# A top-64 attention kernel: exponentials behind the counts, the guess and the moments earlier, a third head copied later

## The reference

```
Q = (layernorm(x) @ Wq.T + bq) by head;  K, V = (ctx @ W.T + b) by head
scores = Q K^T / sqrt(16)
topk_scores, topk_idx = top_k(scores, 64)
attn = softmax(topk_scores) @ V[topk_idx]
x = x + tanh(g_xattn) * (attn @ Wo.T + bo)
x = x + tanh(g_ffn) * (fp8_gemm(layernorm(x)) + bias)
```

## Time and profile before

| | us |
|---|---|
| median of 3 runs | 3224.66 (3223.86 to 3225.97) |
| the profiled execution | 3223.62 |
| its span | 3221.7 |
| VectorE busy | 2552.6 |
| ScalarE busy | 2501.8 |
| TensorE matmul busy | 1510.1 |
| GpSimd busy | 979.2 |

### The profile page before, as it was taken

The page is one execution under the profiler, slowest core; times in us unless marked ns, Lnnn a source line. Parts: engine busy times, 40 slices in busy tenths (PEclk is TensorE's granted clock), DMA queues, the critical chain, the costliest instruction groups (busy, mean ns, idle before and its releaser), DMA issues. The chain is left out here.

```text
span 3221.7 us, 56352 instructions
## 1 busy us (share of the span) xinstructions
PE 1510.1 (47%) x9104; PEld 971.1 (30%) x9104; DVE 2552.6 (79%) x10774; ACT 2501.8 (78%) x8774; POOL 979.2 (30%) x1204
## 2 busy tenths in 40 slices
PE   3244545455444545533545445544454355444442
PEld 2132333233233333322323233323233233232221
DVE  2688788788888788788878888887878887888884
ACT  1777888788888888866888788888788688687892
POOL 6223233223323233322233233223333223232112
PEclk8565666666666666665666666666566666566666
DMA  3223332223333223332223333232333123322211
GB/s 71 47 36 54 57 59 51 49 49 59 64 54 48 55 52 59 55 53 41 49 51 64 54 54 55 53 56 51 63 54 60 34 52 57 53 48 41 41 35 36
DMA packets 451929, 166.76 MB, mean 52 GB/s; under 512 B 245616, under 2 KB 451440, under 8 KB 451520
## 3 DMA queue, kind: packets, MB, share of 16 engines
q1 hardware_dynamic: 451136, 162.38, 28.5%
q0 software_dynamic: 384, 0.33, 0.1%
HBM read 102.57 MB, written 59.24 MB: 50 GB/s over the span
## 5 line engine op out<-in xcount | busy, mean ns | idle before, releaser
L970 ACT ACTIVATE act_junk<-score_sb,X 128x256 int8<-128x256 f32 x3072 | 1521.6, 511 | 52.6 <-DVE X L1272 49.0
L970 ACT ACTIVATION_READ_ACCUMULATOR act_junk<-score_sb,X 128x1 f32 x3072 | 627.7, 204 | 0.0
L1014 ACT ACTIVATE pT_sb<-ps_e 128x512 f32<-128x512 f32 x512 | 304.6, 596 | 400.0 <-PE ps_e L775 400.0
L757 PE MATMUL ps_s<-ks,qs 96*128 96x256 bf16 x1024 | 244.4, 365 | 729.4 <-DVE score_sb L1178 716.8
L1005 ACT ACTIVATE unfit<-score_sb,thr 128x256 bf16<-128x256 f32 x1024 | 430.4, 507 | 149.2 <-DVEq L1443 149.2
L771 PE MATMUL ps_e<-qs,ks 99*128 99x256 bf16 x1024 | 365.4, 365 | 311.2 <-ACT unfit L1005 217.4
L1178 DVE TENSOR_SCALAR_CACHE_REDUCE score_sb<-ps_s 128x256 f32<-128x256 f32 x1024 | 398.1, 411 | 13.4 <-PE ps_s L757 7.8
L775 PE MATMUL ps_e<-dropb,unfit 128*128 128x128 bf16 x2048 | 367.6, 279 | 0.0
L792 PE MATMUL ps_o<-pT_sb,v_aug 128*32 128x256 f32 x2048 | 293.3, 503 | 157.6 <-ACT o_sb L1021 153.2
L567 POOL CAST split<-proj 128x512 bf16<-128x512 f32 x64 | 39.8, 622 | 1000.4 <-ACT proj L954 999.8
L757 PEld LDWEIGHTS ps_s<-ks,qs 96*128 96x128 bf16 x1024 | 100.6, 121 | 782.6 <-DVE score_sb L1178 757.9
(11 more groups left out here) (181 smaller groups left out, 3902.4 us busy)
## 6 DMA issues: line engine op xcount, KB each, us to landing
rows<-q_scr SPq DMA_DIRECT2D x192, 128.0 KB, 5.0
rows<-k_scr SPq DMA_DIRECT2D x192, 128.0 KB, 4.9
o_scr<-o_sb SPq DMA_DIRECT2D x128, 128.0 KB, 2.8
q_scr<-split SPq DMA_DIRECT2D x32, 384.0 KB, 2.7
k_scr<-split SPq DMA_DIRECT2D x32, 384.0 KB, 2.7
x_in<-in_x SPq DMA_DIRECT2D x32, 256.0 KB, 2.8
ctx_sb<-in_ctx SPq DMA_DIRECT2D x32, 256.0 KB, 3.0
v_scr<-proj SPq DMA_DIRECT2D x32, 256.0 KB, 5.9
```

The costliest lines, as they stand in the source:

```text
L757: ins = nc.tensor.matmul(ps_s[:, n % 2, jh * TOK:(jh + 1) * TOK], qs[u][0:SPLITS, h, 8 * jh:8 * jh + 8, :].rearrange("d j t -> d (j t)"), ...
L970: ins = nc.scalar.activation(act_junk[:, t % JUNK, :], score_sb[:, slot, t, :], ACT.Sign, scale=-1.0, bias=X[slot % 2][:, 0, t:t + 1], acc ...
L1014: nc.scalar.activation(pT_sb[:, n % QUAD, :], ps_e[:, n % 2, :], ACT.Exp).then_inc(s_PT, 1)
```

## The change

Four pieces of work move; none is added or removed.

- ScalarE: each third of the counts stands ahead of the round's exponential instead of behind it. The moments are evacuated behind the first third (and its exponential) of round (0,0) instead of behind all three; the guess behind the second third of round 1 instead of ahead of the last third of round 2.
- TensorE: the products of the guess are issued in round 1 instead of round 2, and wait for the moments' evacuation, since both use ps_b. `front_transposes`, which also writes ps_b, waits for the guess's evacuation.
- VectorE: in rounds 0 and 1 the third head's scores are copied behind the update of the thresholds.

```
             def front_transposes(b, taken, estimated):
                 pe.wait_ge(s_xn[0], b + 1)
                 pe.wait_ge(s_mo, taken)
+                pe.wait_ge(s_ge, estimated)
...
                 pe.wait_ge(s_ge, 2 * b + g)
+                pe.wait_ge(s_mo, b + 1)
...
-                        if has(1) and r == 2:
-                            gauss(b + 1, (u + 1) % OPS, g, 2 * b + 6 if has(2) else 2 * NB,
-                                  2 * b + 4 + 2 * g if has(2) else 2 * NB)
+                        if has(1) and r == 1:
+                            gauss(b + 1, (u + 1) % OPS, g, 2 * b + 4, 2 * b + 4 + 2 * g if has(2) else 2 * NB)
...
-                            front_transposes(b + 2, b + 2)
+                            front_transposes(b + 2, b + 2, 2 * b + 3)
...
                     for r in range(GUIDES):
                         for k in range(3):
+                            if guided:
+                                guide_counts(2 * b + g + 1, (2 * p + g + 1) % RING, r, THIRDS[k])
                             if k < len(HEADS[r]):
                                 taken(HEADS[r][k])
-                            elif has(1):
+                            if has(1) and (g, r, k) == (0, 0, 0):
+                                evacuate_moments(b + 1)
+                            if has(1) and (r, k) == (1, 1):
                                 evacuate_gauss(2 * (b + 1) + g)
-                            if guided:
-                                guide_counts(2 * b + g + 1, (2 * p + g + 1) % RING, r, THIRDS[k])
-                        if has(1) and (g, r) == (0, 0):
-                            evacuate_moments(b + 1)
...
                         next(finals)
-                        if not last:
-                            copy(HEADS[r][2], 0)
-                            copy(HEADS[r][2], 1)
                         next(finals, None)
...
                         for _ in steps:
                             pass
+                        if not last:
+                            copy(HEADS[r][2], 0)
+                            copy(HEADS[r][2], 1)
```

More of the change, by code:

```diff
@@ L685, in _, with front_transposes @@
             pe.wait_ge(s_wev, 4)
-            def front_transposes(b, taken):
+            def front_transposes(b, taken, estimated):
                 pe.wait_ge(s_xn[0], b + 1)
                 pe.wait_ge(s_mo, taken)
+                pe.wait_ge(s_ge, estimated)
                 pe.wait_ge(s_ctx, 16 * b + 16)
@@ L835, in _ @@
             for b in range(2):
-                front_transposes(b, 0)
+                front_transposes(b, 0, 0)
                 project(b, 0, 0)
```

## The result

| | before | after |
|---|---|---|
| median, us | 3224.26 (3223.49 to 3225.97, 4 runs) | 3030.81 (3025.43 to 3034.51, 4 runs) |
| ratio | | 0.9398 (0.9382 to 0.9414) |
| span of the profiled execution | 3221.7 | 3032.6 |
| VectorE busy | 2552.6 | 2576.4 |
| VectorE idle (span less busy) | 669.1 | 456.2 |

The change makes the kernel 6.0% faster, 194 us. The prediction's sum was 242 us, to 2983 us, in a range of 2945 to 3090 that holds the measured time. In the two profiled executions VectorE's idle time is 213 us less and its busy time 24 us more.

A forecast was written before the change was run, and what follows sets the result against it. VectorE (79% busy) and ScalarE (78%) were taken to be bound by how they hand work to one another. 99.5 + 81 + 82 - 20 = 242 us saved gives 2983 us; 8 in 10 range 2945 to 3090.

The forecast's parts named there:

- (a): Moments evacuated behind the first third of round (0,0): VectorE's wait for them goes, 99.5 us gained.
- (b): Guess made in the second round instead of the third: VectorE's wait for it goes, less its own handover, 81 us.
- (c): ScalarE's exponentials behind each third of the counts: the last count comes 3.69 + 0.5 us earlier in (0,0).
- The waits for counts: VectorE's waits for ScalarE's counts: 2.7 us a batch go, in 30 batches 82 us.
- my table: One batch followed stretch by stretch in the new order: period 82 us, some 0.9 us of count wait left in (0,2).
- (d): Third head's copy behind the update: new X 0.7 us sooner in four of six rounds, VectorE's own work unchanged.
- Contention: VectorE slowed by GpSimd working beside it: costs 20 us, with bounds of nothing and 60 us.
- the main case: 74% for 2983 us, from 2945 (no contention and no wait left) to 3030 (contention 60).
- Slower: Rival, 5%: later exponentials delay TensorE's first scores of a round, 2 us in each of six rounds, giving 3299 us.
- another ring: Rival, 3%: the keys' projection through ScalarE, GpSimd and DRAM holds the period at 91.6 us; nothing changes, 3224 us.
- Most holes only move: Rival, 18%: waits for ps_e stay on ScalarE behind the counts, so ScalarE sets the period, 86 us a batch; 3073 us.
- the sign against the forecast: ScalarE without a hole in (1,0) and (1,1) while VectorE waits for counts there would show the forecast wrong.

The follow-up runs named there:

- the load on ScalarE: The changed kernel with three of eight exponentials of a half made twice on ScalarE: 3084.97 us, 0.9559 of the kernel before.
- the run with the moves exchanged: The changed kernel with GpSimd's spreading copy in four and, on SyncE, the output's moves ahead of the value rows' moves: 3014.16 us, 0.9334.
- the split kernel: The changed kernel with GpSimd's spreading of an operand by head made as four copies of a quarter: 3013.67 us, 0.9338 of the kernel before.

## Why the prediction was right, and where its sizes were off

- **What bounds the kernel.** Right: the two engines held each other up over ps_e and the moments. The single largest part, by itself 161 us, is the order of counts and exponentials.
- **(a) The moments.** Right: 99.5 us forecast, 98.9 us gone from the wait, 92 us alone.
- **(b) The guess.** The wait went by 81.3 us (idle before `variance`, all causes, 125.2 to 43.9), as forecast. That it is a gain of its own was wrong: alone it gave 8 us, and 55 of the 81 go with (c) alone (125.2 to 70.0). Behind (c), moments and guess together took another 51 us of idle time away (`key_var` 46.0 to 21.2, `variance` 70.0 to 43.9) and gave 19 us back before `X`; in time they are worth some 35 us (3065 to 3028). How much of that is the guess's no run shows.
- **The waits for counts.** Mis-sized: 82 us forecast, 64 measured (idle before `X`, 154.5 to 90.2). In (0,2) a wait of 1.2 us is left for the 0.9 of my table.
- **(c) The order.** It was priced by its waits for counts alone, 82 us, and by itself gave 161 us, since it brings the moments and the guess forward too.
- **(d) The late copy.** This is the step that failed. I wrote "VectorE itself does neither more nor less for it". It costs VectorE 0.15 us for the max and some 0.1 us for the copy, four times a batch: 18 + 16.5 us. The copies had covered VectorE's handovers to itself, and I priced the moved work without asking what it had covered.
- **Contention.** 20 us forecast, 23.8 us measured, and some 33 if the tile that wasn't selected again is counted in (9.4 us). It isn't spread out as I had it: the narrow compares took 49.8 us more and the first step of the update 17.7 us less (55.0 to 37.3).
- **The sum.** 98.9 + 81.3 + 64.3 - 18.1 - 16.5 = 209.9 us of idle time in these groups, and the whole idle time fell by 212.9. Less 23.8 of contention it is 189.1, the difference of the spans. So the sum was nearly right as a sum of waits that go. As a list of what each edit is worth it was not: the edits gave 92, 8, 161 and -35 us alone, and that the total came out has some luck in it, since a wait counted under (b) went with (c).
- **The range.** The lower end, 2945, isn't what stands beside it (3224 - 290 = 2934). The measured 3031 is just above the upper end of the main case, 3030, which was meant for 60 us of contention; it came there by the waits for counts and the late copy instead.
- **The stages.** From the start of the batch to the X of (0,0), 10.1 us forecast, 10.6 measured; (0,1) 15.9 and 16.0; (0,2) 14.4 and 14.6; (1,0) 9.3 and 9.4. Then (1,1), 14.8 forecast, 16.4 measured, and (1,2), 17.6 forecast, 17.4 measured: 1.6 us a batch were missed in (1,1) alone. Read against the batch before, the compares beside GpSimd add 1.9 there and the first step of the update gives 1.0 back; the start of the late copy adds 0.4, line 1497 0.2 and the wait of the max 0.15.
- **The rivals.** "Slower" and "another ring" didn't come: score_sb waits 9.2 us in all for ps_s. "Most holes only move" did in part, for the load on ScalarE still reaches the time by half; but ps_e was not what held it. Of the sign against the forecast, ScalarE without a hole in (1,0) and (1,1) and VectorE waiting for counts there, a part came: (1,0) is full (9.40 of 9.40 us), (1,1) isn't, and VectorE waits for counts in neither.
- **What I hadn't listed.** The output's moves had no slack left: in the changed kernel o_sb starts at 1640.21, behind 0.18 us of waiting for den_sb. By the run with the moves exchanged even the 37.9 us of this wait in the split kernel cost nothing.

Open is why the late score copy of round (1,0) starts up to 0.5 us after the update in some batches; the trace puts a few of these down to ScalarE's masks, which in the code it doesn't wait for at this point, and TensorE had written the scores long before (1680.5 for a copy at 1685.27). No run was made on it.

## What to carry to other kernels

Where two engines are both near 80% busy, look for the wait that stands in front of the others: an instruction that waits for a third engine, ahead of independent work, is worth moving first, and a wait behind another wait for the same engine is worth little until the first is gone (103 us of wait, 8 us of gain). Before an independent instruction is moved, ask what handover it has been covering. And take a wait's price from the run only after you know which engine leads in that stage: adding a known load to each in turn shows it.

## What the runs showed of the hardware

- A two-input instruction of VectorE that meets a GpSimd copy ends just behind it: 3.65 us for two compares of 0.87, beside a copy of 3.60 us; 1.86 us when the copy is made in four. An instruction with one input did so too (line 1260, 0.91 us for 0.18). Splitting the copy spared the compares 44.6 us and cost the instructions behind them 24. GpSimd's time rises by 27.5 us for it (1005.4 to 1032.9) with 192 instructions more.
- VectorE waits for itself: 0.15 us from a compare to the max that reads it, 0.7 us from a score copy with its accumulator to the first instruction of `start_thresholds`, which has four waits ahead of it. Other work between the two covers nearly all of this (0.6 us left before the max, 0.6 before `start_thresholds`, over the whole run).
